# Shared-expert items start three steps later, ten instead of eleven of them ahead of the routed tiles, and the last batch's work is placed anew

## What is computed

```python
x = x + _layernorm(attn(_layernorm(x)))     # 16 query heads, 4 key/value heads of 128, layernorm + rope on q and k,
                                            # causal softmax, output projection
x = x + _layernorm(ffn(_layernorm(x)))

# ffn: 8 experts, each token goes to its top 2, plus one shared expert
probs = softmax(xf @ gate_w.T); weights, indices = top_k(probs, 2); weights /= weights.sum(-1)
h = silu(xf @ w_gate[e]) * (xf @ w_up[e])                    # hidden width 176 per expert
out = sum over the two experts of weight * (h @ w_down[e])
out = out + sigmoid(xf @ shgate_w) * ((silu(xf @ shw_gate) * (xf @ shw_up)) @ shw_down)   # hidden width 352
```

## Time and profile before

| | us |
|---|---|
| median of 3 runs (721.05 to 722.1) | 721.95 |
| the profiled execution | 722.1 |
| its span, first to last instruction | 719.9 |

### The profile page before, as it was taken

The page is one execution under the profiler, slowest core; times in us unless marked ns, Lnnn a source line. Parts: engine busy times, 40 slices in busy tenths (PEclk is TensorE's granted clock), DMA queues, the critical chain, the costliest instruction groups (busy, mean ns, idle before and its releaser), DMA issues.

```text
span 719.9 us, 15495 instructions
## 1 busy us (share of the span) xinstructions
PE 626.6 (87%) x4412; PEld 583.3 (81%) x4412; DVE 565.8 (79%) x1920; ACT 568.9 (79%) x2186; POOL 562.3 (78%) x595
## 2 busy tenths in 40 slices
PE   2567999999999999999999999997688799999840
PEld 2456999989999998998998989997577689999840
DVE  6799988888988988888888899898356665555375
ACT  5869999999989999999999999998654346666433
POOL 5889889999899999999999989998745305666454
PEclk9889999999999999999999999999899899999975
DMA  8002599652000000000000000004123234442342
GB/s 331 1 30 97 162 335 334 173 4 43 1 2 1 2 1 1 1 2 1 1 2 2 1 2 1 1 24 156 67 87 116 91 91 116 122 128 81 138 170 87
DMA packets 50834, 54.20 MB, mean 75 GB/s; under 512 B 19808, under 2 KB 42336, under 8 KB 50624
## 3 DMA queue, kind: packets, MB, share of 16 engines
q1 hardware_dynamic: 47344, 43.84, 21.2%
q0 software_dynamic: 3408, 9.38, 3.5%
HBM read 23.76 MB, written 29.51 MB: 74 GB/s over the span
## 4 chain that ended last, share of the span: by engine, by line
POOL 46%; PE 28%; DVE 13%; issue 7%; ACT 4%; DMA 1%; another core or an unknown queue 0%; SPq 0%; POOLq 0%; ACTq 0%; DVEq 0%
POOL ropes L1705 10%; POOL ropes L1697 10%; POOL ropes L1700 8%; POOL rs L1686 8%; PE pQ L452 3%; PE pQ L454 3%; PE pQ L453 3%; PE pS L452 2%; POOL hrow L1719 2%; POOL osb L1726 2%; POOL lr L1686 2%; PE pS L453 1%; PE pS L454 1%; PE pO L452 1%; PE pS L729 1%
## 5 line engine op out<-in xcount | busy, mean ns | idle before, releaser
L452 PE MATMUL pQ<-W 128*128 128x512 f32 (+2 forms) x334 | 118.3, 354 | 11.2 <-DVE ropes L1207 6.8
L865 ACT ACTIVATE P<-P,nmx 128x128 f32<-128x128 f32 (+1 forms) x256 | 118.6, 490 | 0.6 <-DVE nmx L1228 0.6
L453 PE MATMUL pQ<-W 128*128 128x512 f32 (+2 forms) x334 | 113.9, 341 | 0.0
L454 PE MATMUL pQ<-W 128*128 128x512 f32 (+2 forms) x334 | 113.5, 340 | 0.0
L1697 POOL TENSOR_TENSOR ropes<-ropes 128x640 f32<-128x640 f32 x64 | 100.5, 1570 | 13.0 <-DVE ropes L1207 13.0
L873 ACT ACTIVATE P<-P,rinv 128x128 f32<-128x128 f32 (+1 forms) x256 | 105.6, 480 | 3.7 <-DVE rinv L1234 3.5
L1705 POOL TENSOR_TENSOR ropes<-ropes 128x640 f32<-128x640 f32 x64 | 102.2, 1597 | 5.0
L1238 DVE TENSOR_TENSOR W<-pP,W 128x384 fp32r<-128x384 f32 x128 | 70.4, 550 | 40.2 <-ACT W L878 37.5
L452 PE MATMUL pO<-W 128*128 128x256 f32 x304 | 88.0, 290 | 11.1 <-DVE W L1243 5.6
L850 ACT ACTIVATE ropes<-pQ 128x128 f32<-128x128 f32 x320 | 88.2, 298 | 4.3 <-POOL ropes L1705 4.2
L453 PE MATMUL pO<-W 128*128 128x256 f32 x304 | 86.2, 284 | 0.0
(11 more groups left out here) (234 smaller groups left out, 2231.7 us busy)
## 6 DMA issues: line engine op xcount, KB each, us to landing
xs<-stage SPq DMA_DIRECT2D x1, 17550.0 KB, 58.4
stage<-xs SPq DMA_DIRECT2D x39, 130.0 KB
ropes<-in_ew SPq DMA_DIRECT2D x8, 608.0 KB
stage<-in_wqkv SPq DMA_DIRECT2D x3, 768.0 KB, 8.2
stage<-ys SPq DMA_DIRECT2D x4, 512.0 KB, 6.0
ropes<-ys SPq DMA_DIRECT2D x4, 512.0 KB, 8.1
out<-X SPq DMA_DIRECT2D x8, 256.0 KB, 2.1
X<-in_wo SPq DMA_DIRECT2D x1, 1536.0 KB, 12.7
```

The costliest lines, as they stand in the source:

```text
L452: e.matmul(out, lh, rh, start=start, stop=False, skip_group_check=True)
L453: e.matmul(out, lh, rl, start=False, stop=False, skip_group_check=True)
L454: return e.matmul(out, ll, rh, start=False, stop=stop, skip_group_check=True)
L865: a = e.activation(P[:, z, span(t)], P[:, z, span(t)], ACT.Exp, bias=nmx[:, z, t:t + 1], scale=-1.0, accum_out=sums[:, z, t:t + 1])
```

## The change

Shared items start at step 142 instead of 139, ten of them run ahead of the routed tiles and six behind (eleven and five before); the routed tiles start at step 152. Attention's steps 139 to 141 have no shared item beside them. Batch 6's residual, normalization and logits move one step earlier on all engines. The middle chunk's first and second choice move one step earlier each, its places from step 142 to 138 (TensorE) and 139 (ScalarE, VectorE), with another PSUM bank to hold them. Batch 7's normalization is at step 144 and its logits at 145, the routing of the last chunk at 146, its places at 147, the tile list at 148. GpSimd scatters row tiles 0 to 7 where it did, tiles 8 and 9 at step 141, two transfers ahead of batch 7's second root and two behind, then the middle chunk's eight. The low halves of experts 2 and 3 go to VectorE, those of 6 and 7 to GpSimd. Waits are placed to fit.

```diff
-U0 = 139
-UFIRST = 11
+U0 = 142
+UFIRST = 10
...
-TLAST = U0 + 5
-COUNT = {118: 0, 142: 1, TLAST + 1: 2}
-PLACE = {119: 0, 142: 1, TLAST + 1: 2}
+TLAST = U0 + 3
+COUNT = {118: 0, 138: 1, TLAST + 2: 2}
+PLACE = {119: 0, 139: 1, TLAST + 2: 2}
...
-EHI = {133: 0, 136: 1, 138: 2, 140: 3, 142: 4, 144: 5, 146: 6, 148: 7}
-ELO_D = {143: 4, 147: 5, 148: 6, 149: 7}
-EHALF = {137: 0, 140: 1, 142: 2, 143: 3, 145: 4, 147: 5, 148: 6, 149: 7}
+EHI = {133: 0, 136: 1, 140: 2, 142: 3, 143: 4, 145: 5, 146: 6, 148: 7}
+ELO_D = {141: 2, 143: 3, 144: 4, 148: 5}
+EHALF = {134: 0, 137: 1, 141: 2, 143: 3, 144: 4, 147: 5, 148: 6, 149: 7}
...
-                for (a, b) in CHUNKS for p in (pA,)]
+                for p, (a, b) in zip((pA, pQ[:, 512:1024], pA), CHUNKS)]
...
-                if b == NB - 1:
-                    e.wait_ge(s_placed, 2)
...
                 elif m == 1:
-                    e.wait_ge(s_t2, 2 * NU)
-                    e.wait_ge(s_v, NU)
+                    e.wait_ge(s_placed, 2)
...
-                e.wait_ge(s_aT, min(COUNT_PV[c], NHEAD // 2))
+                if c == 1:
+                    e.wait_ge(s_t2, 2 * NU)
+                    e.wait_ge(s_v, NU)
+                else:
+                    e.wait_ge(s_aT, min(COUNT_PV[c], NHEAD // 2))
...
-                    for x in (3, 7):
+                    for x in (5, 7):
...
-                if q in COUNT and COUNT[q] == 1:
-                    places(1)
...
-                if q in COUNT and COUNT[q] == LASTC:
-                    places(LASTC)
-                    counts()
+                if q in COUNT and q >= U0:
+                    places(COUNT[q])
+                    if COUNT[q] == LASTC:
+                        counts()
...
-                if s == S6 + 8:
+                if s == S6 + 7:
                     ln2_T(NB - 2)
-                if s == S6 + 10:
+                if s == S6 + 9:
                     logits(NB - 2)
...
-                if q == 137:
+                if q == U0 - 3:
                     shared_gate(0, 14)
-                if q == TLAST + 1:
-                    choice(LASTC)
...
-                if q in PLACE and PLACE[q] < LASTC:
+                if q in PLACE:
                     choice(PLACE[q])
...
-                if s == S6 + 9:
+                if s == S6 + 8:
                     ln2_hi(NB - 2)
-                if s == S6 + 11:
+                if s == S6 + 10:
                     logit_lo(NB - 2)
...
-                if s == S6 + 7:
+                if s == S6 + 6:
                     ln2_apply(NB - 2)
...
+                if q == S6 + 10:
+                    route_first_choice(1)
                 if q == S6 + 11:
-                    route_first_choice(1)
+                    route_second_choice(1)
                 if q == S6 + 12:
-                    route_second_choice(1)
-                if q == S6 + 13:
                     route_gap(1)
                     route_count(1)
-                if q == 138:
-                    shared_half(0, 0, 14)
-                    pads()
-                if q == 142:
+                if q == 139:
                     place_read(1)
                     place_own(1)
                     place_ends(1)
-                if q == TLAST:
+                if q == U0 - 2:
+                    shared_half(0, 0, 14)
+                if q == TLAST + 1:
                     route_first_choice(2)
...
-                if q == TLAST + 1:
+                if q == TLAST + 2:
                     place_read(2)
...
-                if q == TLAST + 2:
+                if q == TLAST + 3:
                     tile_list()
-                if q == TLAST + 3:
                     shared_half(1, 14, NT)
...
+                if q == U0 - 1:
+                    pads()
...
-                if s == S6 + 9:
+                if s == S6 + 8:
                     ln2_lo(NB - 2)
-                if s == S6 + 11:
+                if s == S6 + 10:
                     logit(NB - 2)
...
+                if s == S6 + 3:
+                    out_scale(NB - 2)
                 if s == S6 + 4:
-                    out_scale(NB - 2)
-                if s == S6 + 5:
                     out_add(NB - 2)
                     ln2_stats(NB - 2)
...
                     ew_lo(1)
-                    scatter_all(0, 8, 10)
-                    ew_lo(2)
-                if q == 142:
+                if q == U0 - 1:
                     out_root(NB - 1)
-                    ew_lo(3)
+                    scatter_all(0, 8, 9)
                     ln2_root(NB - 1)
+                    scatter_all(0, 9, 10)
                     scatter_all(1, 10, 14)
-                if q == TLAST + 1:
+                    ew_lo(6)
+                if q == TLAST + 2:
                     scatter_all(2, 14, 16)
+                    ew_lo(7)
```

## The result

| | before | after |
|---|---|---|
| median us (4 runs each, one chip) | 721.72 (721.05 to 722.1) | 728.32 (726.65 to 728.8) |
| ratio, 95% interval | | 1.0089 [1.007, 1.0106] |
| the profiled execution | 722.1 | 721.64 |
| its span | 719.9 | 719.6 |

The change makes the kernel 0.89% slower (6.6 us between the medians), where 2.3 us less were forecast. One thing must be kept in mind in what follows: the profiled execution of the changed kernel took 721.6, 5 us less than the fastest of its other runs. What it shows is real, but it is not the whole of the 6.6 us; the study has two more profiles of the same kernel (c1, span 717.3, and d1, span 727.2).

A forecast was written before the change was run, and what follows sets the result against it. TensorE was held to lose 12.9 us to waits and low clock between attention's end and the first routed tile. Terms -3.57 - 0.8 + 0.8 + 1.3 = -2.3 us gave 719.7 as median, range 715.0 to 724.0.

The forecast's parts named there:

- Edits costed at nothing: Middle chunk's places moved earlier, expert low halves swapped between GpSimd and VectorE: zero, else about 0.5 and 1.15 us each.
- Attention's last steps: Batch 6's earlier normalization makes ScalarE wait 2.0 us for GpSimd's root; +1.7 less 0.9 for moved routing, +0.8 us.
- rival D: Attention pays ScalarE's new wait in full: +5.8 in place of +0.8, total +2.7, about 724.7 us; chance 0.18.
- (a): Steps 139 to 141: context copy and low half lie open before the next output projection; 1.2 us lost.
- (b): First shared item's gate waits for its low half, queued on VectorE behind batch 7's statistics; 2.0 us lost.
- (c): First shared item's product stands behind batch 7's scale, add and statistics on VectorE; 2.3 us lost.
- (d): Routing of the last two row blocks: the 1.5 us wait for the one-hots shrinks to 0.7.
- (e): Step 148: VectorE has tile list, a low half and a correction, delaying TensorE's next item; 2.2 us lost.
- (f): Wait ahead of the first routed tile, 1.7 us before, becomes 1.0 as the last low half goes to GpSimd.
- (g): Unexplained lateness in the unbroken run of ten row scatters around batch 7: 2.7 us lost, bounds 0 and 5.
- C: Rival: half clock returns (+1.5) after the gaps, or the sixth item costs 3.57 in full; about 721.5 us; chance 0.22.
- Rival B: Nothing is late in the scatter run, so (g) is 0: -5.0 us, about 717.0; chance 0.20.

The follow-up runs named there:

- c1: The changed kernel unaltered, profiled and timed again: 722.96 us against 711.14 for the kernel before, ratio 1.0162.
- d1: The changed kernel unaltered, a third time: 727.83 us against 722.54 for the kernel before, ratio 1.0066.
- c3: The changed kernel with the low halves of experts 6 and 7 on VectorE at steps 149 and 150: 712.64 us, ratio 1.0022 to before.
- c5: The changed kernel with only expert 6's low half moved to VectorE (step 149): 716.35 us, ratio 1.0069 to before.
- c6: The changed kernel with only expert 7's low half moved to VectorE (step 150): 716.6 us, ratio 1.0072 to before.
- c7: c4 with batch 6's scale, add and statistics back at their old steps, normalization still early: 722.57 us, ratio 1.0000 to before.
- b3: The kernel before with low halves of experts 2 and 3 on VectorE, 6 and 7 on GpSimd: 716.29 us against 711.61, ratio 1.0054.
- b4: The kernel before with only batch 6's residual, normalization and logits one step earlier: 726.74 us against 723.16, ratio 1.0051.
- b1: The kernel before, unaltered, profiled once more: 709.0 us in a single execution; its other runs on that chip have median 711.61.
- c8: c7 with the rest of batch 6's chain and the middle chunk's routing a step later: 718.64 us against 723.16, ratio 0.9943.
- c4: The changed kernel with the edits of c2 and c3 together: 712.84 us, ratio 1.0022 to before.
- d3: d2 with eleven shared items ahead of the routed tiles and five behind, still from step 142: 721.97 us, ratio 0.9993 to before.
- d2: c8 measured a second time: 718.84 us, ratio 0.9951 to the kernel before, which took 722.5 beside it.
- b2: The kernel before with ten shared items ahead; experts 5 to 7's low halves and corrections a step earlier: 725.07 us, ratio 1.0033.
- c2: The changed kernel with expert 0's half correction back at step 137 and expert 1's at 138: 723.4 us, ratio 1.0159 to before.

## Why the prediction was wrong

The forecast was 2.3 us faster; the runs give 6.6 and 5.3 us slower on chips where before takes 722, and 11.8 where it takes 711. Beside the earlier trace rows, d1 divides its +7.3 us of span so: last probabilities 530.07 for 526.43, +3.6, forecast +0.8; from there to the first routed tile 63.1 for 60.4, +2.7, forecast -4.4; the rest +0.9, forecast +1.3.

*The step that failed most: "Edits costed at nothing".* It put the low halves of experts 6 and 7 on GpSimd at zero, or 1.15 each. Together they cost 10 us where before takes 711 (c1 against c3; c5 and c6 for each alone). Where before takes 722, which is where the forecast was made, no run moved them alone; c7, which takes both away with expert 0's correction and the early scale, is 0.66 to 0.89% under the changed kernel (d1, and the first measurement), 4.8 to 6.4 us for all of it, and d1 shows the two waits, 3.3 for the one-hots and 4.85 behind the list. The error is in kind: the cost was sought on VectorE's queue, which they leave, and not in what GpSimd's 2.2 us subtraction does to a VectorE instruction beside it. The prediction cited the row and the rule for that very thing, in the tail: the Trainium skill (SBUF - State Buffer, Who interferes with whom) says that a VectorE instruction reading two SBUF operands contends with a GpSimd one that reads SBUF. The L1371 rows with 2.87 and 0.17 us agree, and the rule should have been held against each GpSimd instruction that the change moves. The same passage put the low halves of experts 2 and 3 on VectorE at nothing; b3 shows that this isn't free, and for the changed kernel its price stays open.

*Attention's last steps, +0.8.* They cost 3.6 us in d1 and 4.0 in b4, where this is the only edit. Where before takes 711 the slip is longer: the last probabilities are at 518.2 and 518.5 in b1 and b3 and between 523.8 and 526.6 in c1 to c6, 5.3 us and more later. That is rival D in its outcome: a slip near 2.7 us at step 132 that nothing takes back. Two points of my working failed. The slip came from the scale of batch 6, of which I had not followed the new place (ahead of a head's reciprocal on VectorE); the wait of 2.0 on ScalarE was real, but shown only with the scale moved back (c7), and undoing the rest gives another 4.1 us (c8). And the "late answer" did not absorb the slip (d1). D's price, 5.8, is near what both parts are worth by the ratios: 0.79% from c4 to c8, across two chips, some 5.7 us; b4 measures 3.6 for the chain alone.

*One item fewer ahead, -3.57, and one more behind, +1.3.* Right: -2.3 forecast, -3.1 measured (d3 against d2), and the tail grew by 0.9 to 1.8.

*(a) to (f).* Four of six were about right where the two GpSimd subtractions are out. In c3 (a) is 1.4 for 1.2; (b) 1.9 for 2.0; (d) 0.48 for 0.7, but 3.15 with expert 6 beside it; (e) 1.95 for 2.2, but 3.94 with expert 7. (c) is 0.4 in c3 and 0.4 to 1.5 in all of them, for 2.3; (f) is 0.43 for 1.0. Together c3 idles 6.6 us, where (a) to (f) were put at 9.4. The stretch of c3 against b1 is 51.1 for 56.0, -4.9, and that this is near the forecast's -4.4 is luck: the -4.4 has 2.7 for (g) in it, which is absent in both, and c4, with the same waits, has 54.5. In both the first routed tile opens 3.5 to 4.1 us later than in b1, since the last probabilities are later still.

*(g), and the half clock.* The gap of 3.9 us was followed by a low clock (0.72 for 6 us), so C's condition came true through gaps that I had not forecast. The late answers are absent in every profile taken where before takes 711, present in every one where it takes 722 but the first one of the changed kernel. Rival B's condition holds in that execution, and even so it was not faster (721.64 for 722.1). Between the two kinds of chip the kernel before differs by 11 us and the changed kernel by 5 (728 for 723), and so the same change costs 0.7 to 0.9% on one and 1.6% on the other. That the late answers make this difference is likely and not shown.

*Three sums of the prediction.* The slip of the copy at 497.84 is given as 1.96 + 1.09 = about 2.7; the sum is 3.05, and 2.7 comes out only if the 0.40 of idle time ahead of that copy is taken off. The sign turns once attention's tail is 3.1 us later than before (3.57 + 0.8 - 1.3), not 4.5; 4.5 is where slower could be told from no change. And B with the tail fully hidden is 717.0 - 1.3 = 715.7, not 715.0.

The account by the ratios, where before takes 711: low halves +1.40% (c1 to c3), batch 6's chain with the middle chunk's routing +0.79% (c4 to c8, the latter on another chip), the rest of the change -0.57% (c8) or -0.49% (d2): 1.62 to 1.70 against 1.62 measured. This is not a check, since each term is a difference to the next kernel and c3 and c4 are equal: such a sum must come out. What it says is that the change without those two parts is 3.5 to 4.1 us faster than before where before takes 722, as far as the forecast's sum without its attention term, -3.1. So the late shared items do win about what was hoped of them, and more was given away twice by edits that looked free.

What stays open: what the late answers are. No kernel here takes them away by its own doing, and every kernel here keeps such long runs of scatters, so it isn't shown either that the scatters are what makes them; they go with the chip, or with the hour. And why b2 loses 1.9 where d3 against d2 wins 3.1: b2 also moved weights a step earlier, which no run tried by itself.

## What to carry to other kernels

Work that is moved to GpSimd is not off VectorE's hands: a large two-operand subtraction there (2.2 us here) holds the VectorE instruction that meets it until it ends, as a rule one with two inputs, so place it where VectorE has nothing on the path, and cost it by its own length, not by what VectorE is spared. When an edit is put into another kernel to price it, check in the trace that the loss begins where the edit's suspect stands: in b3 most of it began before. A sum of differences from kernel to kernel always comes out, and proves nothing. Where a change advances a chain, follow each instruction of the chain to its new neighbours; two delays in one chain can hide one another, and undoing one of them then shows little. When a kernel's ratio differs between chips, compare only within a chip, and check that the profiled execution is a usual one before reading a sum from it.

## What the runs showed of the hardware

- An instruction of VectorE beside GpSimd's 128x960 subtraction (2.2 us) took 2.87, 2.11 (the changed kernel), 2.64 (c5), 2.89 (c6) and 2.80 us (d1) where its twins took 0.17 to 0.28. It ended within 0.1 us of GpSimd's. Four of these five rows begin 0.35 to 0.6 us before GpSimd's row. A pair of adjoining GpSimd subtractions (1.83 and 2.21) held a 64x256 correction for 4.24 us instead of 0.42.
- A VectorE reduction with one input took its usual 0.18 us inside such a subtraction (c2), and an instruction with two inputs behind it was held. Of instructions with one full SBUF input the 128x39 TENSOR_SCALAR was held too (2.11 and 2.80).
- The 128x256 pair of TENSOR_SCALAR with one full SBUF input took 2.33 to 2.46 beside GpSimd's rope work, in the kernel before as well, and 1.17 without it.
- The kernel before differs by 1.6% between chips (711 and 722). Where it takes 722, ScalarE or VectorE starts up to 3.8 us late, with nothing in the trace that releases it, in or just behind runs of eight or more row scatters; TensorE and the other engine then wait behind the late one (up to 5.5 us). The Trainium skill (SBUF - State Buffer, Who interferes with whom) states that "PE and ACT never wait on anyone"; the rows where before takes 711 agree, the others don't show the opposite, since a port is not the only thing that could be late.
